# Four graph layers in one kernel: neighbour sorts with one operand held in PSUM, staging on SyncE, and paired window words

## What is computed

```python
edge_index = jnp.stack([src, dst])            # 12500 nodes, 400000 edges, dst sorted in the input
x = _layernorm(x + _L0_gnn_ref(x, edge_index, ...))   # attention, 4 heads: segment_max, exp, segment_sum over src
x = _layernorm(x + _L1_gnn_ref(x, node_vec1, ...))    # partial convolution: segment_sum(w * v[dst], src)
x = _layernorm(x + _L2_gnn_ref(x, edge_weight, edge_attr_3, ...))  # per edge: radial net x spherical harmonics x x[src], added at dst
x = _layernorm(x + _L3_gnn_ref(x, edge_index, ...))   # two graph convolutions with relu, segment_sum at dst

# inside L0:
e = leaky_relu(a_src[:, src] + a_dst[:, dst] + fc_b[0], 0.2)
e = jnp.exp(e - segment_max(e.T, src).T[:, src])
att = e / segment_sum(e.T, src).T[:, src]
agg = segment_sum(att[:, :, None] * hp[:, dst, :], src)
```

## Time and profile before

| | us |
|---|---|
| median of 3 runs | 22574.52 |
| lowest and highest of them | 22572.42 and 22581.99 |
| the profiled execution | 22578.48 |
| span of the profiled execution | 22576.5 |

### The profile page before, as it was taken

The page is one execution under the profiler, slowest core; times in us unless marked ns, Lnnn a source line. Parts: engine busy times, 40 slices in busy tenths (PEclk is TensorE's granted clock), DMA queues, the critical chain, the costliest instruction groups (busy, mean ns, idle before and its releaser), DMA issues.

```text
span 22576.5 us, 289421 instructions
## 1 busy us (share of the span) xinstructions
PE 9970.0 (44%) x63545; PEld 7520.1 (33%) x63546; DVE 17227.1 (76%) x23890; ACT 4905.7 (22%) x12809; POOL 14764.3 (65%) x14067
## 2 busy tenths in 40 slices
PE   0123101101005777542224887878788864226422
PEld 0122001001004666531123555555555543224321
DVE  8999999999718888631565999999999975664566
ACT  0000000000001222231001444444444444004300
POOL 0048888788765777777775777777766621770376
PEclk9755555555557888755555888888888865555555
DMA  2001111211221111384233111111100056235524
GB/s 47 0 16 24 23 26 22 30 24 24 32 39 37 35 35 35 64 165 85 66 73 43 12 12 12 12 12 12 12 11 11 11 108 186 71 69 155 157 71 63
DMA packets 1837590, 1095.97 MB, mean 49 GB/s; under 512 B 988875, under 2 KB 1789100, under 8 KB 1836076
## 3 DMA queue, kind: packets, MB, share of 16 engines
q0 software_dynamic: 454272, 412.11, 12.6%
q1 hardware_dynamic: 886268, 362.30, 6.6%
q10 hardware_dynamic: 496944, 320.42, 5.8%
HBM read 700.94 MB, written 391.12 MB: 48 GB/s over the span
## 4 chain that ended last, share of the span: by engine, by line
POOL 36%; issue 19%; DVE 19%; DVEq 13%; PE 10%; DMA 2%; ACT 1%; POOLq 0%; SPq 0%; ACTq 0%
POOL gat L745 18%; POOL pay L711 13%; DVEq L2307 9%; POOL srcs L765 5%; DVE srcs L2302 5%; PE banks L1272 3%; PE banks L1330 3%; DVE hot L2020 3%; DVE red L2308 3%; DVE arena L1651 2%; DVE srcs L2297 1%; DVEq L487 1%; PE banks L1317 1%; DVE arena L2031 1%; DMA srcs<-spread,nbx 1%
## 5 line engine op out<-in xcount | busy, mean ns | idle before, releaser
L745 POOL DMA_INDIRECT gat<-tab,nbr x3328 | 4265.9, 1282 | 2336.4 <-DMA nbr<-nbr_src 1322.3
L765 POOL DMA_INDIRECT srcs<-spread,nbx x2808 | 3094.1, 1102 | 2480.2 <-DMA nbx<-from_src 1615.1
L745 POOL DMA_INDIRECT gat<-tab,pay x3328 | 3164.3, 951 | 1078.1 <-issue 867.9
L711 POOL DMA_INDIRECT pay<-records,nbr x2784 | 3034.9, 1090 | 1091.2 <-issue 848.3
L1330 PE MATMUL banks<-w2rows,dsts 128*128 128x384 f32 x6656 | 3236.6, 623 | 854.8 <-DVE srcs L2302 683.5
L2308 DVE TENSOR_REDUCE red<-srcs 128x80 f32<-128x1280 f32 x1664 | 2474.7, 1487 | 151.5
L1191 PE MATMUL banks<-srcs,hot 128*128 128x96 bf16 (+1 forms) x11232 | 1148.3, 278 | 3264.1 <-DMA srcs<-spread,nbx 3171.8
L1120 PE MATMUL banks<-ident,arena 128*128 128x128 f32 x2240 | 427.9, 377 | 4532.0 <-DVE arena L1652 4508.1
L2031 DVE TENSOR_TENSOR arena<-arena,banks 128x96 f32 (+2 forms) x4472 | 1210.4, 271 | 1358.8 <-issue 888.1
L1651 DVE TENSOR_TENSOR arena<-arena 128x1024 f32<-128x1024 f32 (+3 forms) x1548 | 2087.7, 1349 | 78.5 <-issue 3.0
L1652 DVE TENSOR_TENSOR arena<-arena 128x1024 f32<-128x1024 f32 (+3 forms) x1548 | 2100.0, 1357 | 0.0
(11 more groups left out here) (377 smaller groups left out, 19345.3 us busy)
## 6 DMA issues: line engine op xcount, KB each, us to landing
spread<-srcs SPq DMA_DIRECT2D x936, 192.0 KB
dsts<-key_rows SPq DMA_DIRECT2D x936, 128.0 KB
spread<-srcs ACTq DMA_DIRECT2D x468, 204.0 KB
staged<-gat ACTq DMA_DIRECT2D x416, 148.0 KB, 1.8
gat<-staged ACTq DMA_DIRECT2D x416, 148.0 KB
dsts<-key_rows ACTq DMA_DIRECT2D x468, 128.0 KB
gat<-tab,nbr POOLq DMA_INDIRECT x3328, 2.5
gat<-tab,pay POOLq DMA_INDIRECT x3328, 2.4
```

Source lines behind the costliest of these rows:

```text
L711: pool.indirect_dma_start(out=pay[:, s, t, :], out_offset=None, in_=records, in_offset=bass.IndirectOffsetOnAxis(ap=nbr[:, s, t:t + 1], ax ...
L745: pool.indirect_dma_start(out=gatv(s, GC[pas])[:, t, :], out_offset=None, in_=TAB[pas], in_offset=bass.IndirectOffsetOnAxis(ap=row, axis=0 ...
L765: pool.indirect_dma_start(out=chunk_rows(s, c)[:, q, :], out_offset=None, in_=rows, in_offset=bass.IndirectOffsetOnAxis(ap=nbx[:, s, q:q + ...
```

## The change

It has these parts.

1. **Held operands.** In the sorts k = 1 to 5, ACT copies the first operand of a round, in two parts, from SBUF to PSUM (`hold`, `sort_operands`), and DVE's minimum and maximum read it there and the second operand in SBUF (`exchange_held`). The rounds that start a stage or a merge, the rounds that end an exchange across rows, and the whole sort k = 0 keep both operands in SBUF. A held merge round is four instructions of a quarter row. The drains between held rounds are gone; DVE waits for `operand_held`, ACT for `operand_set`.
2. **The last round of a merge** tells PE of each half as it is done (`sorted_in` by 1 twice); before, it told of both at its end.
3. **Staging on SP.** `stage` and `neighbour_load` move from ACT to SP. The copy into `adst_c` is dropped: the attention terms are stored from `gat` directly, in pieces of 16 bytes. The loads and stores of keys and numbers that SP issued between sorts move to ACT.
4. **Lanes in PSUM.** `place_lanes` copies `iota` to PSUM bank 7 once a pass, and `one_hot` reads it there (attention and collecting passes).
5. **Window words for pairs.** `win_src` and `win_nbr` hold packed words; spreading and collecting steps read one word of four numbers for two steps.
6. **Numbers early.** `nbx` is a ring of three, each with the numbers of four steps, loaded by one DMA; POOL waits for PE's sums of the step four before instead.

```diff
             def chunk_number_loads(pas, numbers):
-                with sp.Fori(0, XITERS) as i:
-                    for s in range(SLOTS):
-                        sp.wait_ge(step_done, i * SLOTS + (BASE[pas] + s + 1))
-                        sp.dma_start(nbx[:, s, :], numbers[:, bass.ds(i * (SLOTS * XGPS) + s * XGPS, XGPS)]).then_inc(nbx_in[s], 16)
+                size = SLOTS * XGPS
+                with sp.Fori(0, KEY_ITERS) as i:
+                    for r in range(RING):
+                        first = i * (RING * size) + r * size
+                        sp.wait_ge(step_done, i * KEYS + (BASE[pas] + (r + 2 - RING) * SLOTS))
+                        sp.dma_start(nbx[:, r, :], numbers[:, bass.ds(first, size)]).then_inc(nbx_in[r], 16)
...
+            def stage(i, final):                          # on SP
+                for s in range(SLOTS):
+                    n = i * SLOTS + s
+                    sp.wait_ge(gat_in[PASS_MAX][s], gat_count(PASS_MAX, i))
+                    sp.dma_start(staged_v[:, bass.ds(i * (SLOTS * TPS) + s * TPS, TPS), :],
+                                 gat[:, s, :, :]).then_inc(staged_out[s], 16)
+                    if not final:
+                        neighbour_load(i + 1, s)
+                        sp.dma_start(adst_tiles[:, bass.ds(n * (TPS * HEADS), TPS * HEADS)].rearrange("p (t h) -> p t h", t=TPS),
+                                     gat[:, s, :, F + 1:C0]).then_inc(adst_out[s], 16)
...
-                        pool.wait_ge(nbx_in[s], i * 16 + (16 * k * XITERS + 16))
+                        pool.wait_ge(nbx_in[r], i * 16 + (16 * k * KEY_ITERS + 16))
+                        for s in range(SLOTS):
+                            pool.wait_ge(sums_ready, i * KEYS + (SUMS_BASE[pas] + r * SLOTS + s + 1 - SLOTS))
...
+            def hold(part, log, first, ahead=1):          # on ACT
+                set_count[0] += ahead
+                act.wait_ge(operand_set, set_count[0])
+                s_.copy(sort_held(part, log, first), first).then_inc(operand_held, 1)
...
+            def exchange_held(src, dst, log, bit, low, up, done):      # on DVE
+                for part in range(2):
...
+                    dve.wait_ge(operand_held, held_count[0])
+                    held = sort_held(part, log, a[:, d, 0, :, :, :])
+                    v.tensor_tensor(b[:, d, e, :, :, :], held, a[:, d, 1, :, :, :], ALU.min)
+                    last = v.tensor_tensor(b[:, d, 1 - e, :, :, :], held, a[:, d, 1, :, :, :], ALU.max)
+                    if done:
+                        last.then_inc(done, 1)
...
+            lanes_p = bank[7][:, 0:P]
...
-                return v.tensor_tensor(dst, iota[:, :].rearrange("p (a n) -> p a n", a=1).to_broadcast([P, TPS, P]),
+                return v.tensor_tensor(dst, lanes_p.rearrange("p (a n) -> p a n", a=1).to_broadcast([P, TPS, P]),
...
-                    wins = windows(win_tab, n, XGPS)
+                    if s % 2 == 0:
+                        pair[:] = windows(win_tab, i * (SLOTS // 2) + s // 2)
```

More of the change, by code:

```diff
@@ L482, in resnorm_gnn_kernel, with group_windows @@
         PE_ENGINE, DVE_ENGINE, ACT_ENGINE = mybir.EngineType.PE, mybir.EngineType.DVE, mybir.EngineType.Activation
-        def group_windows(eng, which, win_tab, n, groups):
-            if groups < GPS:
-                _, vals = nc.values_load_multi_w_load_instructions(
-                    win_tab[0:1, bass.ds(n * groups, groups)], engines=(which,), min_val=0, max_val=W - 1,
-                    skip_runtime_bounds_check_because="the table is clamped to W - 1 where it is made")
-                return vals
+        def group_windows(eng, which, win_tab, n):
             _, (word,) = nc.values_load_multi_w_load_instructions(
@@ L497, in group_windows, with sort_pairs, sort_half, sort_held @@
             return fields
+        def sort_pairs(t, bit, low, up):
+            return t.rearrange("p (x d m two l) -> p d two x m l", d=1 if up else 2, m=1 << (bit - low - 1), two=2, l=1 << low)
+        def sort_half(t, log, half):
+            return t[:, half << (log - 1):(half + 1) << (log - 1)]
+        def sort_held(part, log, like):
+            _, x, m, l = like.shape
+            lo = part << (log - 1)
+            return flat[:, lo:lo + (1 << (log - 2))].rearrange("p (x m l) -> p x m l", x=x, m=m)
         GEO_OPS = 3
@@ L611, in _ @@
             sp.dma_start(nbr_src, sortB[:, 0:NT].bitcast(I32)).then_inc(nbr_sent, 16)
-            sp.wait_ge(rows_ended, 1)
-            with nc.allow_non_contiguous_dma(reason="one key per row"):
-                sp.dma_start(prev_key[1:P, :], sortB[0:P - 1, M - 1:M].bitcast(I32)).then_inc(prev_in, 16)
-            sp.wait_ge(listed, 2)
-            sp.dma_start(ids_dst, sortA[:, 0:NT].bitcast(I32)).then_inc(ids_sent, 16)
-            for k in range(2):
-                sp.wait_ge(row_keys_made, k + 1)
-                sp.dma_start(key_rows[k].rearrange("(p g) c -> p (g c)", p=P), row_keys).then_inc(row_keys_sent, 16)
+            sp.wait_ge(nbr_sent, 16)
+            for s in range(SLOTS):
+                neighbour_load(0, s)
+            stage(0, False)
+            with sp.Fori(1, ITERS - 1) as i:
+                stage(i, False)
+            stage(ITERS - 1, True)
             sp.wait_ge(ids_sent, 16)
@@ L878, in _ @@
-            act.wait_ge(nbr_sent, 16)
-            for s in range(SLOTS):
-                neighbour_load(0, s)
-            stage(0, True, False)
-            with act.Fori(1, ITERS - 1) as i:
-                stage(i, False, False)
-            stage(ITERS - 1, False, True)
+            act.wait_ge(rows_ended, 1)
+            with nc.allow_non_contiguous_dma(reason="one key per row"):
+                act.dma_start(prev_key[1:P, :], sortB[0:P - 1, M - 1:M].bitcast(I32)).then_inc(prev_in, 16)
@@ L1702, in sort @@
                                     last.then_inc(sorted_in, 1)
+                                elif k and low > 1:
+                                    last.then_inc(operand_set, 1)
                         elif low == 0:
```

215 lines of the change are left out of this document (141 added, 74 removed).

## The result

| | before | changed |
|---|---|---|
| median | 22573.47 | 21501.72 |
| lowest and highest | 22571.01, 22581.99 | 21499.03, 21504.47 |
| span of the profiled execution | 22576.5 | 21498.9 |

The account below looks back on a forecast made before the run. POOL's gathers beside the sorts were taken to bound the first stage, DVE's step the collecting passes. Gains of 670 (first stage), 270 (collecting passes) and 40 (spreadings), 980 us, took 22575 to 21600; range 21430 to 21880.

Parts of the forecast that it names:

- Gathers beside the sorts: In the sorts, POOL's gathers beside held rounds come every 1.25 us instead of 1.63; POOL ends near 5845.
- DVE's sorts: Held rounds without drains and shorter waits for PE save 100 us; DVE's sorts end near 5997 instead of 6097.
- The sign to look for: In the sorts, a wait of 1.5 instead of 3.77 us after a merge, written as PE waiting.
- The rule on PSUM operands: DVE's held instructions in the sorts cost 65 ns more each, 196 us, about 21800; left out of the sum; chance 10%.
- Staging on SP: Beside the sorts' gathers, 16-byte pieces at 27 ns per packet take 1.7 us per step, hidden under 10 us; nothing counted.
- My threshold of 13.4 us: Staging step time, 200 ns per packet, at which slower pieces also eat the other parts' 310 us; chance 3%.
- The sum of this stage: From the start to the segment maximum's load: it starts at about 5999 instead of 6668.8, 670 us gained, DVE last.
- The attention pass: Gains nothing: POOL stays at four gathers per step, whether or not the one-hot tile holds it.
- The rival at 12%: POOL gets faster in the attention pass too, by some 5%, worth 100 us: 21500; chance 12%.
- The collecting passes: DVE's step sets the pace; fewer window loads save 90 us a pass, 270 for three, bounds 40 and 130 per pass.
- The spreadings: First gains nothing; in the other two PE reads its windows in pairs, 20 us each, 0 to 60.
- the fast rival: POOL gets faster in the attention pass too, 100 us, giving 21500; chance 12%.

Follow-up runs that it names:

- m1: Changed kernel with held rounds reading SBUF, first-pass lanes in SBUF, single window loads in second spreading (PE) and second collecting pass (DVE): 22664.72 us, ratio 1.003.
- m3: Changed kernel with PE told once after a merge, attention terms stored twice, numbers of the collecting passes loaded per step: 21617.75 us, ratio 0.9577.
- m2: Changed kernel with held-round drains back, single window loads in first and third collecting pass and third spreading, lanes in SBUF in second and third pass: 21970.34 us, ratio 0.9734.
- e4: Changed kernel, but in the attention pass ACT writes the probabilities to PSUM, where DVE's message tile reads them: 21213.17 us, ratio 0.939 to the kernel before.
- e1: Changed kernel with DVE reading the first operand of held rounds in SBUF, on two other chips: 27443.41 us, ratio 0.9878, and 27886.22 us, ratio 0.988.

## Why the prediction was right, and where not

**Gathers beside the sorts: right.** The step was that one free SBUF operand frees POOL at 1.25 us. The changed kernel shows it and m1 takes it away with that operand alone. POOL's end, put at 5845, was 5868 for its last gather and 5878 for the last store.

**DVE's sorts: right in kind, 36 us short.** Forecast 100 us, measured 136. The waits behind PE gave 65 (79.1 + 28.9 to 31.0 + 12.1, the two sizes apart) where I had 73, and m3 puts them down to the halves told early. (The sign to look for was written as PE waiting; it is DVE that waits for PE, at most 1.5 us behind a merge, as I had put it.) The waits for ACT cost 23, in 25 places, where I had 26 in 25. The term mis-sized most is the pitch of a held instruction: 1.13 us from start to start, 4.52 for four, where I put 4.57; over 158 rounds in three sorts that is 24 us. Another 9 I gave away by taking 100 for a sum of 109. A merge round without its drain (0.20 us by m2) but with two instructions more gains these 0.05 us too, where I had nothing. An ACT copy of 1024 took 1.05 us of my 1.0 to 1.6, one of 512 took 0.60, and both fit.

**The rule on PSUM operands** that I had set aside (the Trainium skill, "VectorE: DVE Perf Modes", trn2 errata: 120 cycles against 58, by my estimate 65 ns more per instruction) doesn't show here either. In m1 the same instructions with both operands in SBUF start 1.13 to 1.14 us apart, and the sorts end 36 us later, not 196 earlier. The rows without any gather beside them say the same: in the kernel before, at 698.94 to 702.35 us with POOL idle, instructions of 1024 elements on two SBUF operands start 1.14 us apart, and with one in PSUM the changed kernel has 1.13.

**Staging on SP: right that it is hidden, wrong in size and place.** I took an average of 27 ns per packet and got 1.7 us per step for the pieces. The step's DMA time grew by 2.7 us (2.3 to 5.0), and some 2.2 of it is the gathers' own packets (1.7 to 3.9 us per step by the queues' shares below), a term that I did not have; the staging's queue grew by only 0.4. A second set of pieces took another 5.3 and brought the engines to 98%. My threshold of 13.4 us was not reached by either.

**The sum of this stage** put DVE last with POOL behind it by 150 us; it is 82 to 92. Forecast 670, measured 708: the 38 us more are DVE's but for 2.

**The attention pass: right.** Four gathers per step before and after. The rival at 12% (POOL faster by 5%) didn't come, and e4 shows why: with the one-hot tile free, the message tile makes the train, and with that gone too the gain is 277 us.

**The collecting passes: right in the sum, with half of the reason left out.** Forecast 270, measured 263, tiles 2.1 and 3.0 us apart as said. Single passes gained 110, 68 and 85 against 90 each, so that the sum came out within 7 us is luck. I counted the gain as DVE's fewer window loads, and gave the lanes in PSUM only a clause on POOL's floor. The table of m1 and m2 shows that the pairs alone would have lost some 60 us or more a pass. With them and the lanes in SBUF a gather costs 1.20 us busy and 0.30 of issue, 3.0 us per step; DVE, which needs 2.63, then waits for PE and PE for POOL's rows. In the kernel before, POOL stood at 2 x (1.12 + 0.30) = 2.84 us beside the 2.81 that DVE takes in m2 with the same loads: the two were level, and only both edits moved the pass far. I had that row and reckoned POOL's floor only for the kernel after. Why a held gather costs 1.20 us with the pairs and 1.12 without them was not tried. That the second pass gained less than the first has part of its place at its end: over its last 100 us a step takes some 3.3 us with the DMA engines at 86% and 58 GB/s, and in the kernel before it is the same at 79% and 57 GB/s; no edit touches it.

**The spreadings: too small.** 65 and 42 against 20 and 20, in the bounds for one of them. m1 and m2 put 37 us in each down to PE's one word for two steps. The other 28 us of the second spreading are open: it ran at 71 steps per 100 us before and at 74 in m1 with the same loads.

**The total.** 1078 us between the spans against 980: 38 more in the sorts, 67 in the spreadings, 7 less in the collecting passes. That the fast rival's 21500 is the number measured is chance: what it said of the attention pass did not happen.

## What to carry to other kernels

Ask of each long DVE instruction how many operands it reads in SBUF before asking how long it is; moving one of two to PSUM, by an idle engine, freed POOL at no cost to DVE. Where two engines stand within a few per cent of each other, an edit to one can be worth little alone, or lose, so price both and measure all four combinations. Before small pieces go to a queue, ask what they do to the packets of the others in that stretch; the queue's own average does not tell.

## What the runs showed of the hardware

- A GpSimd gather beside back-to-back DVE instructions on two SBUF operands locks to every second of them: 2.27 us each beside instructions 1.135 us apart (e1, m1), 1.25 with one operand in PSUM. The sorts' DVE work ends 36 us later (m1, 3016 such instructions).
- Beside stores of 16-byte pieces another queue's packets take longer. A gather's packet took 106 ns in the sorts before (13.0% of 16 engines over 3997 us, 78688 packets), 242 ns beside 128 x 8 pieces a step in the changed kernel, 314 ns beside twice as many in m3. The gathers' faster rate is not the cause: at that rate without such pieces (before, 6100 to 6650 us, the last row) a packet took 112 ns.

```profile
q0 software_dynamic: 78688, 46.74, 13.0%
```

```profile
q0 software_dynamic: 92759, 55.09, 37.3%
```

```profile
q0 software_dynamic: 92437, 54.91, 47.7%
```

```profile
q0 software_dynamic: 14112, 8.38, 18.0%
```

- Chips differ for this program. The kernel before takes 22570 to 22595 us in five sets of runs, and 27782 and 28240 us on two other chips, there too within 0.4% from run to run. Why was not found.
